# Field-pair projection on one Trainium2 core: one first load instead of two, six weight pieces instead of seven, three first stores instead of four

## The reference

```python
PAIRS = np.array(list(combinations(range(32), 2)))
xi = x[:, PAIRS[:, 0], :]
xj = x[:, PAIRS[:, 1], :]
proj = jnp.einsum('bpd,pod->bpo', xi, W)   # W: (496, 64, 64)
return proj * xj                            # (2048, 496, 64), float32
```

## Time and profile before

| what | us |
|---|---|
| median of three runs | 669.47 |
| the profiled execution | 670.16 |
| its span, from the first instruction to the last | 668.4 |
| PE busy | 577.2 (86%) |
| POOL busy | 419.1 (63%) |
| DVE busy | 410.9 (61%) |
| ACT busy | 232.1 (35%) |

### The profile page before, as it was taken

The page is one execution under the profiler, slowest core; times in us unless marked ns, Lnnn a source line. Parts: engine busy times, 40 slices in busy tenths (PEclk is TensorE's granted clock), DMA queues, the critical chain, the costliest instruction groups (busy, mean ns, idle before and its releaser), DMA issues.

```text
span 668.4 us, 7464 instructions
## 1 busy us (share of the span) xinstructions
PE 577.2 (86%) x2704; PEld 340.8 (51%) x2704; DVE 410.9 (61%) x528; ACT 232.1 (35%) x301; POOL 419.1 (63%) x256
## 2 busy tenths in 40 slices
PE   5998989989898998979979898898989979799930
PEld 4565555545455554645545455465555645456510
DVE  0776666856566665665856566465666756567630
ACT  2334334343333334333243333233334243433400
POOL 0866848585765866757585774666748575656720
PEclk9999999999999998998999999798999999999975
DMA  8999999999999999999999999999999999999997
GB/s 347 436 437 427 435 422 433 439 429 429 437 429 430 432 433 426 443 433 428 428 431 433 426 432 436 433 427 432 424 428 436 434 429 423 444 423 437 440 424 321
DMA packets 11257, 285.15 MB, mean 427 GB/s; under 512 B 1776, under 2 KB 1904, under 8 KB 2672
## 3 DMA queue, kind: packets, MB, share of 16 engines
q1 hardware_dynamic: 8496, 270.27, 94.1%
q0 software_dynamic: 2464, 14.68, 5.2%
q10 hardware_dynamic: 288, 0.08, 0.1%
HBM read 25.56 MB, written 260.05 MB: 427 GB/s over the span
## 4 chain that ended last, share of the span: by engine, by line
DMA 55%; PE 22%; POOL 7%; DVE 6%; issue 3%; ACT 2%; SPq 0%; DVEq 0%; ACTq 0%; POOLq 0%
DMA out_dram<-staged 37%; PE proj L378 19%; DMA x_in<-x_dram,rows_sb 18%; DVE staged L427 6%; POOL staged L301 6%; PE proj L356 3%; ACT staged L343 2%; DMA ident_sb<-ident_dram 1%; PE proj L400 1%; POOL x_in L283 0%; POOL x_in L274 0%; ACT x_t L328 0%; SPq L248 0%; DVEq L424 0%; ACT x_sb L321 0%
## 5 line engine op out<-in xcount | busy, mean ns | idle before, releaser
L378 PE MATMUL proj<-w_sb,x_t 64*128 64x512 f32 (+7 forms) x2432 | 540.1, 542 | 43.0 <-ACT staged L343 26.8
L427 DVE TENSOR_TENSOR staged<-proj,x_sb 128x1024 f32<-128x1024 f32 (+7 forms) x528 | 410.9, 826 | 231.5 <-PE proj L378 199.9
L301 POOL TENSOR_TENSOR staged<-staged,x_sb 128x1024 f32<-128x1024 f32 (+4 forms) x224 | 390.5, 1756 | 215.3 <-ACT staged L343 211.1
L378 PEld LDWEIGHTS proj<-w_sb,x_t 64*128 64x128 f32 x2432 | 307.9, 190 | 260.0 <-issue 123.8
L343 ACT ACTIVATE staged<-proj 128x1024 f32<-128x1024 f32 (+4 forms) x224 | 171.3, 786 | 323.4 <-PE proj L378 267.0
L321 ACT ACTIVATE x_sb<-x_in 128x2048 f32<-128x2048 f32 x14 | 26.7, 1910 | 68.5 <-DMA x_in<-x_dram,rows_sb 68.5
L356 PE MATMUL proj<-ident_sb,x_sb 128*128 128x128 f32 x256 | 37.1, 292 | 14.3 <-DVE staged L427 14.3
L356 PEld LDWEIGHTS proj<-ident_sb,x_sb 128*128 128x128 f32 x256 | 29.6, 148 | 33.2 <-DVE staged L427 27.3
L328 ACT ACTIVATE x_t<-proj 128x512 f32<-128x512 f32 (+1 forms) x62 | 34.7, 609 | 13.1 <-PE proj L356 13.1
L283 POOL DMA_INDIRECT x_in<-x_dram,rows_sb x14 | 14.5, 1036 | 3.0 <-issue 1.3
L274 POOL DMA_INDIRECT x_in<-x_dram,rows_sb x14 | 13.9, 991 | 2.5 <-issue 2.5
## 6 DMA issues: line engine op xcount, KB each, us to landing
out_dram<-staged SPq DMA_DIRECT2D x16, 5504.0 KB, 24.4
out_dram<-staged SPq DMA_DIRECT2D x15, 5472.0 KB, 24.9
out_dram<-staged SPq DMA_DIRECT2D x16, 4896.0 KB, 25.3
out_dram<-staged SPq DMA_DIRECT2D x1, 3520.0 KB, 16.6
w_sb<-w_dram SPq DMA_DIRECT2D x1, 2944.0 KB, 21.3
out_dram<-staged SPq DMA_DIRECT2D x1, 1952.0 KB, 12.8
w_sb<-w_dram SPq DMA_DIRECT2D x1, 1664.0 KB, 12.1
w_sb<-w_dram SPq DMA_DIRECT2D x1, 1408.0 KB, 14.9
```

The source lines that it names most:

```text
L301: last = nc.gpsimd.tensor_tensor(product, product, x_sb[tile.parity][:, j * dim:(j + n) * dim], ALU.mult)
L378: last = nc.tensor.matmul(proj[b][h][:, at:at + width], x_t[half, turned_at(i, fields), :], w_sb[half, col:col + width], start=True, stop= ...
L427: last = nc.vector.tensor_tensor(staged_part(item, i, j, n), proj[b][h][:, at:at + n * dim], x_sb[tile.parity][:, j * dim:(j + n) * dim], ...
```

## The change

The first tile's x is one load. The second of the cuts that divided the matrices falls out: 512 columns and the 960 behind them become one piece of 1472, so six pieces are left. `FIRST_MERGED` equals `MERGED`, so the first tile stores slot 0 with one transfer. PE and DVE wait on one semaphore for the first x.

```diff
-FIRST_MERGED = [[0], [1, 2], [3, 4, 5, 6], [7, 8, 9, 10]]
+FIRST_MERGED = MERGED
...
-    w_cuts = [0, BANK] + [ends[s] for s in (0, 1, 3, 7, 11)] + [w_end]
+    w_cuts = [0, BANK] + [ends[s] for s in (1, 3, 7, 11)] + [w_end]
...
-        x_first_loaded = [sem(f"x_first_loaded{h}") for h in range(2)]
+        x_first_loaded = sem("x_first_loaded")
...
-            half = fields * dim // 2
-            sp.dma_start(x_sb[0][:, 0:half], x[0:P, 0:half]).then_inc(x_first_loaded[0], 16)
+            sp.dma_start(x_sb[0][:], x[0:P, :]).then_inc(x_first_loaded, 16)
             sp.dma_start(w_sb[:, w_cuts[0]:w_cuts[1]], w_block(0)).then_inc(w_loaded[0], 16)
-            sp.dma_start(x_sb[0][:, half:], x[0:P, half:]).then_inc(x_first_loaded[1], 16)
...
+            pe.wait_ge(x_first_loaded, 16)
             for h in range(2):
-                pe.wait_ge(x_first_loaded[h], 16)
                 turn(0, 0, h, 0, fields // 2)
...
                 if tile.first:
-                    for h in range(2):
-                        dve.wait_ge(x_first_loaded[h], 16)
+                    dve.wait_ge(x_first_loaded, 16)
```

## The result

The kernel after has a median of 672.82 us, beside 669.98 us for the kernel before on the same chip (16 runs each): a ratio of 1.0042, 95% interval 1.0026 to 1.0059. It is slower by 2.8 us. The forecast was +2.8 us, by one hole of 3.1 us near 27 us, less 0.3. The size came true. The place did not: in the profile that hole is much smaller and paid for by quicker loads, and the loss that all DMA engines share arises at 40 to 44 us.

The account below looks back on a forecast made before the run. DMA transfers were taken to bound the kernel; a hole of 26.71 + 0.5 + 3.3 - 27.4 = 3.1 us, less 0.3, moved the median from 669.47 to 672.3 us, range 669.7 to 673.4.

Parts of the forecast that it names:

- A hole in the transfers is not made up: Whole run: DMA engines are busy without a gap from 40 to 660 us, so time with nothing to move is lost.
- The merged store is what costs, the loads cost nothing: Start of run: the merged store leaves a 3.1 us hole; fewer, larger loads have cost and gain zero.
- L: Time from a store's issue to its first packet, at the merged first store; taken as 3.3 us.
- The low end: Lower bound for L, from the very first load on an idle machine: about 1.0 us.
- s: Shift of the first tile's compute chain because the identity lands later: 0.5 us, bounded by nothing and 1.2 us.
- Whatever the loads gain only makes the hole longer at its front: Near 27.4 us: loads may finish sooner, but the compute chain sets the store's issue; cost and gain zero.
- store starts at once: Rival at the first store: L is 1.0 us, net loss 0.5 us, 670.0 us; chance 0.38 including nearly at once.
- third rival: Second hole, in tile 1: the third tile's x lands over 3 us later, delaying a store; 674.5 us, chance 0.06.
- late engine: An engine running late enters the hole near 27.4 us later and loses less: 0.3 us off, bounds 0 and 1.
- The sum: Hole near 27 us: 26.71 + 0.5 + 3.3 - 27.4 = 3.1 us, less 0.3, giving 2.8 us.
- largest late store: Upper end of the late-store case (chance 0.52): L 3.3, s 1.2, deduction 0, given as 673.6 us.
- slower by more than that: Whole run: chance 0.60 of being slower by more than 1.3 us, what a measurement can tell from no change.

Follow-up runs that it names:

- e6: Kernel after with the first tile's slot 0 store held back until POOL has done group 3, two steps later: 676.45 us, ratio 1.0097.
- e2: Kernel after with the first tile's slot 0 stored in two transfers again, one load of x and six weight pieces kept: 669.61 us, ratio 1.0010.
- e8: Kernel after with the store in two and the first tile's five-row indirect load issued earlier: 670.54 us, ratio 0.9999.
- e1: Kernel before with only the first tile's store merged; x in two loads and seven weight pieces stay: 670.83 us, ratio 1.0026.
- e7: Kernel after with the first x in two halves again; merged store and six weight pieces stay: 670.99 us, ratio 1.0012.
- e4: Kernel after with the first tile's large indirect load moved behind POOL's work for the second slot: 672.97 us, ratio 1.0058.
- e5: Kernel after run again with no edit: 672.64 us, ratio 1.0039.
- e9: Kernel before with the first tile's five-row indirect load issued one step later, some 2.4 us: 671.98 us, ratio 1.0034.
- e3: Kernel after with the first tile's five-row indirect load issued some 6 us earlier, merged store kept: 671.29 us, ratio 1.0027.
- e10: Kernel after with the first x in two halves and the first tile's five-row load issued earlier: 671.82 us, ratio 1.0028.
- e11: The kernel of e10 run once more, unchanged: 671.21 us, ratio 1.0019.

## Why the prediction was right in size and wrong in place

- **A hole in the transfers is not made up: right.** e6 shows it with a hole of known size, and from 60 to 660 us every kernel runs at 430 to 432 GB/s. (The last is a weak check: those 2 GB/s over 600 us are 2.8 us.)
- **The merged store is what costs, the loads cost nothing: right, with a reserve.** e2 and e8, the kernel after with the store in two, are at 1.0010 and 0.9999, with intervals that hold 1; all kernels with the merged store are above, 1.0012 to 1.0097. Without the single load of x the merged store costs 1.0026 (e1) and 1.0012 (e7), with it 1.0042 and 1.0039. Whether the single load adds to it there is not settled.
- **L, the term that was mis-sized.** I took 3.3 us from issue to first row. It was 0.85 us. The low end, 1.0 us from the very first load, was the right row. The reading of the earlier trace rows failed at the step "if the store had been ready before 42.25 it would have shown". e4 is the test: issued ahead of the x rows, the store followed the one before without a gap. In the kernel before the store was issued 1.3 us before the first rows of x moved and had yet to stand behind most of them. There the Trainium skill's rule ("DMA: Bandwidth & Descriptors", section "Queues, rings and completion order": an engine drains a run of descriptors of one queue before it turns to the next) fits better than the one-for-one turns that I drew from the earlier trace rows. The trace shows both patterns, at different times; what decides between them is open.
- **s: the cause right, the size within bounds, but luck is larger.** The identity landed 0.57 us later (6.58 against 6.01 us; 6.22 to 6.45 in the other kernels with one x, 5.85 to 6.02 in those with two halves). But the start of step 0 was 12.91 against 13.29, since the warm-up took 3.38 us instead of 3.67 and the transposes of x 1.91 us instead of 2.61 (in e5 3.19). The profiles of one and the same kernel differ by more than s: 26.25 and 27.40 us for this store's issue.
- **"Whatever the loads gain only makes the hole longer at its front": right, and I left out what it means.** The hole opens earlier because the same bytes are done earlier, so the part of it at its front is no loss. By 40 us the kernel after was level in spite of its hole of 0.3 us; e5, with one of 1.3 us, was behind by 3 GB/s times 40 us, 0.3 us.
- **The rival "store starts at once" had nearly the right L, 1.0 us, and gave +0.5 us, 670.0 us; the missing 2.3 us are the thin stretch and what comes behind 60 us.** The thin stretch was no part of any case. The third rival looked at the same x rows, but one tile on. The sum asked for the store's own waiting, and that rival for the landing of the large load; neither asked what the merged store's longer rows do to the five-row load that was queued beside it, and who waits for that. The row was there: POOL issues the small load 0.1 us behind SP's store and needs it landed before the large one.
- **The late engine.** I took 0.3 us off for it. It went the other way: in the profiled pair the last engine fell behind by 2 us more (shares at the end, above). The mean of the engines accounts for 1.5 of the 3.7 us between the two spans, the latest engine for the rest.
- **Two slips in the prediction's numbers.** Its largest late store, L 3.3 and s 1.2 without deduction, is 26.71 + 1.2 + 3.3 - 27.4 = 3.8 us, so 673.3 us, not 673.6. And "slower by more than that" can be 0.58 at most, 0.52 and 0.06, not 0.60. Neither moves the forecast.

So the agreement of 2.8 us with 2.8 us is luck: two errors that made up for each other, a hole too large by 1.8 us (e5) to 2.8 us (the kernel after), and a thin stretch with a late engine that was not in the sum.

What is shown and what is not: the merged store makes the loss (the kernel after and e5 against e2 and e8). How it does so is shown in part. POOL's wait for the small load can make a loss of this size (e9 makes the wait in the kernel before and gets 1.0034; the kernel after has it in both profiles). It is not all of it: without it e3 had a thin stretch, and e10 and e11, without that stretch, keep 0.2 to 0.3%. Why rows of x take 0.54 us in some stretches and 0.31 in others was not settled. Two readings come to mind, that POOL's indirect load hands its rows out too slowly for engines that have nothing else, and that sixteen engines which read x at one moment slow each other. Neither is enough by itself: in 40.25:42.25 the kernel before moved 83 rows of x beside 0.06 MB of stores, and they took 0.31 us each.

No version beat the kernel before; e8 equals it.

## What to carry to other kernels

When transfers bound a kernel, count the bytes moved up to a few marks, before and after, and look for the loss where the two part; the busy share can hide it (0.97 here at half the rate), since an engine holding a slow row counts as busy. A transfer made larger can delay the small ones that share its engines (here from 7.7 to 9.9 us), so ask who waits for the small ones, above all an engine that issues further transfers behind that wait. And a sum that agrees with the clock proves nothing about its terms; undo one part at a time before believing it.

## What the runs showed of the hardware that was not expected

- From a store's issue to its first row with engines that had run out of work: 0.85 us (26.25 to 27.10 in the kernel after; 27.40 to between 28.20 and 28.40 in e5), less than the 1.0 us of the first load of the program.
- A row of 8192 bytes from memory through POOL's indirect queue took 0.31 us in the kernel before and 0.54 us in the kernel after, both times where nearly nothing but such rows moved (40.25:42.25 and 42:43.6).
- One transfer of x with 8192-byte rows filled the ramp better than two with 4096-byte rows: 266 against 216 GB/s in 1.8:4 us and 382 against 342 in 4:6. In all profiles: 258 to 290 against 216 to 233, and 375 to 402 against 293 to 342.
- The 16 transposes of x, with the same granted clock of 1.00 in the records, took between 1.91 and 3.19 us from one execution to the next (272 ns each in the kernel after, 421 ns for most of them in e5), which shifts the first tile's whole chain.
